# Mixing and base matmuls one tile further behind the attention, in code written out slot by slot

## What is computed

```python
# block 1: a low-rank adapter chosen per sample, then autocorrelation attention
u = einsum('bni,bri->bnr', x, B[id]); v = einsum('bnr,bor->bno', u, A[id])
f = rfft(v); corr = irfft(f * conj(f), n=1024)
weights, delay = top_k(corr, 6)                  # per row, over the 1024 lags
x = x + sum_k softmax(weights)[k] * roll(v, -delay[k])
# block 2: a 64x64 mix of the channels, chosen per sample, then a base layer with LoRA experts
m = einsum('bct,bcd->bdt', x, W[cond])
out = x + m @ W_base.T + b_base + 2.0 * top2_of_8_lora_experts(m)
```

## Time and profile before

| | us |
|---|---|
| median of 3 runs | 948.55 |
| lowest, highest | 946.2, 956.33 |
| span of the profiled execution | 948.1 |
| PE busy in it | 839.0 |
| DVE busy | 620.8 |
| POOL busy | 478.5 |
| ACT busy | 336.3 |

### The profile page before, as it was taken

One profiled execution on the slowest core, in us unless ns is written; L12 is line 12 of the kernel. 1 busy time (PEld: TensorE's weight loads), 2 busy tenths in 40 slices (PEclk: granted clock), 3 DMA queues, 4 the chain that ended last, 5 costly groups with the idle time before them and its releaser, 6 DMA issues. The chain is left out here.

```text
span 948.1 us, 16004 instructions
## 1 busy us (share of the span) xinstructions
PE 839.0 (88%) x4808; PEld 705.7 (74%) x4808; DVE 620.8 (65%) x1362; ACT 336.3 (35%) x617; POOL 478.5 (50%) x465
## 2 busy tenths in 40 slices
PE   4646899998998998998988989989989989999978
PEld 3645788777777787777877877777867778778766
DVE  2245667867677676766677576766667766777772
ACT  5343334233433333333442334333333333333311
POOL 1244544746575552755556355655337544555530
PEclk9856999999999999999999999999999989999998
DMA  8466576676766776665767667667666667777441
GB/s 277 140 195 203 185 232 213 211 239 197 232 201 203 237 240 185 212 217 184 234 202 242 192 195 214 194 208 226 193 209 194 206 212 223 234 235 234 166 146 45
DMA packets 66796, 194.48 MB, mean 205 GB/s; under 512 B 13708, under 2 KB 24236, under 8 KB 63540
## 3 DMA queue, kind: packets, MB, share of 16 engines
q0 software_dynamic: 23040, 83.90, 28.1%
q1 hardware_dynamic: 32084, 71.33, 26.8%
q10 hardware_dynamic: 11616, 38.67, 10.4%
HBM read 118.36 MB, written 50.33 MB: 178 GB/s over the span
## 5 line engine op out<-in xcount | busy, mean ns | idle before, releaser
L1093 POOL DMA_INDIRECT rolled<-y_d,off x160 | 168.6, 1054 | 297.9 <-DVE row L939 191.0
L939 DVE SCALAR_TENSOR_TENSOR row<-rolled,weight,row 128x1024 f32<-128x1024 f32 x160 | 226.5, 1416 | 101.7 <-DMA rolled<-y_d,off 98.6
L463 PE MATMUL o_ps<-wt_hi,x_hi 128*128 128x512 f32 x512 | 219.6, 429 | 0.0
L463 PE MATMUL o_ps<-wt_hi,x_lo 128*128 128x512 f32 x512 | 202.2, 395 | 0.0
L463 PE MATMUL o_ps<-wt_lo,x_hi 128*128 128x512 f32 x512 | 201.7, 394 | 0.0
L1082 POOL TENSOR_TENSOR row<-row,bias 128x1024 f32<-128x1024 f32 x32 | 77.7, 2427 | 88.1 <-PE x_ps L570 88.1
L570 PE MATMUL x_ps<-mix,row 128*128 128x128 f32 x512 | 76.5, 311 | 50.5 <-DVE row L939 32.6
L570 PEld LDWEIGHTS x_ps<-mix,row 128*128 128x128 f32 x512 | 70.4, 220 | 63.4 <-DVE row L939 38.2
L463 PEld LDWEIGHTS o_ps<-wt_hi,x_hi 128*128 128x128 f32 x512 | 96.6, 189 | 22.5 <-issue 4.8
L463 PEld LDWEIGHTS o_ps<-wt_hi,x_lo 128*128 128x128 f32 x512 | 96.2, 188 | 22.1
L463 PEld LDWEIGHTS o_ps<-wt_lo,x_hi 128*128 128x128 f32 x512 | 97.0, 189 | 14.6
(11 more groups left out here) (130 smaller groups left out, 1485.5 us busy)
## 6 DMA issues: line engine op xcount, KB each, us to landing
y_d<-y ACTq DMA_DIRECT2D x64, 512.0 KB, 3.6
row<-in_x SPq DMA_DIRECT2D x32, 512.0 KB, 7.0
adapter<-g_hi SPq DMA_DIRECT2D x64, 256.0 KB, 4.5
out<-row SPq DMA_DIRECT2D x32, 512.0 KB, 2.9
adapter<-g_lo SPq DMA_DIRECT2D x32, 256.0 KB, 4.5
r<-in_L_cond_A SPq DMA_DIRECT2D x72, 64.0 KB
r<-in_L_cond_B SPq DMA_DIRECT2D x56, 64.0 KB, 2.0
rolled<-in_L_ffn_W_base SPq DMA_DIRECT2D x5, 512.0 KB, 6.0
```

The lines of the kernel that those rows point to most:

```text
L463: last = pe.matmul(dst, a, b, start=start and n == 0, stop=stop and n == len(todo) - 1)
L939: dve.scalar_tensor_tensor(row[u][:, :], rolled[n % RB][:, :], weight[:, n:n + 1], row[u][:, :], ALU.mult, ALU.add).then_inc(sum_step, 1)
L1093: pool.indirect_dma_start(out=rolled[n % RB][:, :], out_offset=None, in_=y2_d[u], in_offset=bass.IndirectOffsetOnAxis(ap=off[:, n:n + 1], ...
```

## The change

LAG becomes 3. `base`, `experts`, `router`, `bias_added`, `out_add` and the store work on tile s-3. `mixed` and its copies work on m = s-2, where they stood on s-1. All keep their places in the slots, so `mixed(s-2)` stands where `mixed(s-1)` stood, in front of `correlation(s)`. There is one slot more, 34. A fifth row buffer holds the tile that is now kept longer, tile t in buffer t % 5. Its space comes from `ft`, which now lies in `r2`. The loop goes: all 35 slots are written out on all five engines, with constants in the waits. `load_mix` gets a wait on `x2_mm` of four tiles before.

```diff
-LAG = 2
+LAG = 3
 U = 4
+NROW = 5
...
-def wait_apart(eng, regs, holds, *waits):
...
-        row = [sb(f"row{u}", [P, L]) for u in range(U)]
+        row = [sb(f"row{n}", [P, L]) for n in range(NROW)]
...
+        ft = r2[:, 0:L].rearrange("p (k c) -> p k c", k=KC)
...
-        ft = sb("ft", [P, KC, P])
...
-        def slots(eng, slot):
-
-            for s in range(U):
-                slot(s, s % U, s // U)
-            with eng.Fori(1, NG - 1) as i:
-                for u in range(U):
-                    slot(i * U + u, u, i)
-            for s in range(NT - U, NT + LAG):
+        def slots(slot):
+            for s in range(NT + LAG):
                 slot(s, s % U, s // U)
...
             def load_mix(t, u):
+                if t >= U:
+                    sp.wait_ge(x2_mm, 2 * (t - U) + 2)
...
             def slot(s, u, i):
-                t, g = s - LAG, i + 1
+                t, m, g = s - LAG, s - LAG + 1, i + 1
...
-                if has(s - 1):
+                if has(m):
                     if prep and u == 0:
                         pe.wait_ge(at_out, 2 * g + 2)
...
-                    mixed(s - 1, *before(u, i, 1))
+                    mixed(m)
                 if attn:
                     correlation(s)
...
-                if has(last):
+                if has(m):
                     for h in range(2):
-                        act.wait_ge(x2_mm, 2 * last + 1 + h)
+                        act.wait_ge(x2_mm, 2 * m + 1 + h)
...
-                if has(last):
+                if has(m):
                     for h in range(2):
-                        dve.wait_ge(x2_h, 2 * last + 1 + h)
+                        dve.wait_ge(x2_h, 2 * m + 1 + h)
```

More of the change, by code:

```diff
@@ L239, in tiles @@
         b_in = sem("b_in")
-        row_in = [sem(f"row_in{u}") for u in range(U)]
+        row_in = [sem(f"row_in{n}") for n in range(NROW)]
         mix_in = [sem(f"mix_in{u}") for u in range(U)]
@@ L450, in _ @@
             load_a(1)
-            slots(sp, slot)
-            for u in range(U):
-                sp.wait_ge(out_saved[u], 16 * NT // U)
+            slots(slot)
+            for n in range(NROW):
+                sp.wait_ge(out_saved[n], 16 * len(range(n, NT, NROW)))
         @blk.tensor
@@ L620, in slot @@
                         base(t, c)
-                    if c < 2 and attn and not first(s):
-                        x_transposed(s, u, i, c)
-                    if c == 2 and attn and not first(s):
+                    if c < 2 and attn and s > 0:
+                        x_transposed(s, c)
+                    if c == 2 and attn and s > 0:
                         b_times_x(s, u, i)
@@ L626, in slot @@
                         pe.wait_ge(x2_l, 2 * t + 2)
-                    if c == (6 if first(s) else 2) and u == 0 and prep:
+                    if c == (6 if s == 0 else 2) and u == 0 and prep:
                         a_transposed(g)
@@ L630, in slot @@
                         h_transposed(t)
-                    if c == 3 and attn and not first(s):
+                    if c == 3 and attn and s > 0:
                         bx_repeated(s)
@@ L644, in slot @@
                         adapter_out(s, u)
-                    if first(s) and c in (4, 5):
+                    if s == 0 and c in (4, 5):
                         w_transposed(KC - 6 + c)
@@ L694, in _ @@
             pe.wait_ge(g_lo_sp, 1)
-            slots(pe, slot)
+            slots(slot)
         @blk.scalar
@@ L776, in slot @@
                                    accum_out=rsum[:, :]).then_inc(rexp_out, 1)
-                if attn and not first(s):
+                if attn and s > 0:
                     x_out(s, t)
-                if prep and u == 0 and not first(s):
+                if prep and u == 0 and s > 0:
                     a_out(g)
@@ L874, in _ @@
             w_high(5)
-            slots(act, slot)
+            slots(slot)
         @blk.vector
         def _(dve):
-            regs = [dve.alloc_register(f"dve_wait{n}") for n in range(2)]
             def low(dst, src, hi):
@@ L998, in slot @@
                     weights(last)
-                    add_y(last, ul)
-                if has_attn(s) and not first(s):
+                    add_y(last)
+                if has_attn(s) and s > 0:
                     bx_masked(s)
                 if has(last):
-                    add_rolled(last, ul, 0)
+                    add_rolled(last, 0)
                 if has(t):
@@ L1006, in slot @@
                     low(ht_lo[:, :], ht_ps, ht_hi[:, :]).then_inc(ht_l, 1)
-                if has_attn(s) and not first(s):
+                if has_attn(s) and s > 0:
                     stack_low(s)
-                if first(s):
+                if s == 0:
                     w_low(KC - 2)
@@ L1046, in _ @@
             w_low(5)
-            slots(dve, slot)
+            slots(slot)
         @blk.gpsimd
         def _(pool):
-            regs = [pool.alloc_register(f"pool_wait{n}") for n in range(3)]
             for u in range(U):
@@ L1137, in _ @@
             pool.wait_ge(bias_in, 16)
-            slots(pool, slot)
+            slots(slot)
 _INS = ["x", "itok_B_4_50", "itok_B_0_15", "L0_cond_A", "L0_cond_B", "L0_cond2_weights", "L0_ffn_W_base",
```

170 lines of the change are left out of this document (84 added, 86 removed).

## The result

| | us |
|---|---|
| after, median of 4 runs | 971.65 |
| lowest, highest | 967.8, 978.21 |
| before, beside it, median of 4 runs | 950.45 |
| after / before | 1.021, interval 1.016 to 1.026 |
| span of the profiled execution | 972.8 |

The change makes the kernel 2% slower. The prediction was 950, with a range of 928 to 961.

The account below looks back on a forecast made before the run. Bound: a ring of correlation, `top_delays`, gathers and rolled additions, with POOL's `powers`, `eo_hi`, `eo_lo` beside; PE's list nearly as long. Terms -13.0 - 1.0 + 1.1 + 0.6 + 4.2 - 2.8 - 1.2 + 13.9 = +1.8 gave 950 us, range 928 to 961.

Parts of the forecast that it names:

- the collision: POOL's bias addition, released sooner, runs before DVE's `eo_lo` instead of beside it and holds it up, 2.2 us.
- what would show it: Signs: no "issue" wait before L899, wait moved to `c_ps`, `eo_lo` some 3 us in slots 14, 18, 22, 26.
- Rival A: The idea works: `eo_lo` gets in before the bias addition; -20.7 us, 928 us, chance 0.22.
- Jumps and register waits, "-13.0 - 1.0": Written-out code removes DVE's stalls after five jumps, -13.0 us, and register waits before the first gather, -1.0 us.
- Rival C: DVE's "issue" stall isn't the jump's and stays in written-out code; 963 us, chance 0.05.
- Rival B: Written-out code stalls in its own instruction fetches, 2.7 us each; 1036 us at one a slot; chance 0.07.
- POOL isn't there earlier; nothing: Slots with u = 0: `folds` stands between `powers` and the bias addition, so no change.
- u = 2, "31.3 each, +1.1" and "slot 10 stays": Five slots with u = 2: 31.3 us each with 0.2 for the clock, +1.1 in all; slot 10 unchanged, `eo_lo` late anyway.
- Slots 28 to 31, "+4.2, between 0 and 8.4": Last slots without preparation: bias addition holds `eo_lo`, +2.1 us in slots 28 and 30; +4.2, between 0 and 8.4.
- u = 3, "+0.6": Slots with u = 3: slot 11 gives 0.6 us, slot 23 loses 1.2 by the bias addition holding `eo_lo`; +0.6.
- Front, "-2.8 - 1.2": Slot 1 loses its mixing, -2.8 us; slot 2 loses `base`, -1.2 us.
- Tail, "+13.9": One slot more after the last correlation: 56.8 us for 42.9, with 0.8 for the clock; +13.9 (+13 to +15).

Follow-up runs that it names:

- e2: Changed kernel with one more wait: POOL's bias addition goes behind `eo_lo`; 940.74 us, ratio 0.988 to the kernel before.
- e3: Changed kernel with a bias addition of one column instead of 1024; 938.68 us, ratio 0.987 to the kernel before.
- e1: Changed kernel with LAG = 2 again: written-out code and fifth buffer without the lag; 946.44 us, ratio 0.995 to the kernel before.
- e5: e2 with one more wait: DVE's last rolled addition waits until POOL's `powers` are done; 943.48 us, ratio 0.989 to the kernel before.
- e10: e9 with LAG = 2, so the same three orders without the lag; 914.27 us, ratio 0.959 to the kernel before.
- e7: Changed kernel with bias addition and `a_low` behind `eo_lo`, and last rolled addition behind `powers`; 932.0 us, ratio 0.978 to the kernel before.
- e9: e7 with the last rolled addition held behind `powers` only in slots with u = 1; 924.28 us, ratio 0.972 to the kernel before.
- e8: e1 with the last rolled addition waiting until POOL's `powers` are done; 942.62 us, ratio 0.990 to the kernel before.
- e4: Changed kernel with 26 unread transposes between mixing and correlation in six slots with u = 2; 963.64 us, ratio 1.012 to the kernel before.

## Why the prediction was wrong

**Where it failed.** The path and the collision that were forecast are the ones that came. What failed are sizes, two above all: the gain of the written-out code, put at -14.0, measured -5.9, and slots 28 to 31, put at +4.2 and at most 8.4, measured +11.5. Behind several terms stands one more, the clock after an idle stretch, allowed 0.2 a slot with u = 2, 0.8 in the tail and nothing elsewhere, and measured at 0.8 and 2.65 in the first two.

**The mechanism held.** The row was read rightly: the bias addition, released sooner, goes ahead of `eo_lo`, which takes 2.95 in slots 6, 10, 14, 18, 22 and 26; the wait moves to `c_ps`, as what would show it said; DVE has no "issue" wait over 0.3. e2 and e3 show that this is the cause. The rule of the Trainium skill, "GPSIMD Engine Reference", Specifications, that GpSimd shares its SBUF interfaces with VectorE and is contended by instructions with two SBUF inputs, agrees with all of these rows (2.95 against 0.81); the section says nothing on who goes first, and this alone is worth 31 us. Rival A is half right in this light: its order, forced by e2, is better by far than the forecast's, but it gave 941 and not 928: by the slots some 8 of the jumps' gain are missing, to which the second collision belongs, and 4.5 with u = 3.

**Jumps and register waits, "-13.0 - 1.0".** Mis-sized: u = 0 and u = 1 together gave -5.9. The stalls did vanish, 11.7 us in e1. Rival C fell with that.

Rival B fell too: in the changed kernel no "issue" wait of DVE or POOL is over 0.3. PE has one of 1.95 before its first mixing, in slot 2, in every kernel with LAG = 3; it wasn't looked into and is far from one a slot. Three of the other written-out kernels have a long one of POOL in front of a gather: 5.3 in slot 29 of e2 and e5, 7.75 in slot 23 of e10. They delay nothing: the same gather starts at 11.5 us of slot 29 there and at 11.3 in the kernel before, and at 13.8 of slot 23 in e10 and in the kernel before, where the profile puts its wait down to a rolled addition. Slot 23 is longer than its like in every kernel: 26.0 to 27.7 in the one before, the changed one and those with LAG = 2, 27.9 to 31.5 in e2 to e7 and e9, where the others with u = 3 mostly take 24 to 25. Why it grows in these stays open.

Two things took the gain back. The gathers, 0.47 us sooner, were priced "-1" with a lower bound of 0; an earlier start was taken to be no loss at worst. In e1 the slots with u = 1 came to +4.2, by the collision with `powers` that e5 and e8 take away again and by the clock in some of them. (In the changed kernel they came to -1.7.) And with the lag mixing is done early in the slots with u = 0 as well, PE idles before the correlation, and in four of them (4, 8, 12, 20) it then takes 2.8 to 3.3 where it took 1.9. Slot 4, "25.5" before, took 28.7: 1.4 by this, and 1.8 because its last rolled addition started 1.4 later, took 2.22 for 1.82 against POOL's folds, and `eo_lo` ended at 25.2 of the slot and not at 23.4. The prediction put these slots down as "POOL isn't there earlier; nothing": it looked at POOL and not at the clock.

**u = 2, "31.3 each, +1.1" and "slot 10 stays".** +3.2 in the five slots (158.6 for 155.4) and +1.9 in slot 10. The collision's 2.2 was right; where 0.2 had been allowed for the clock, 0.8 was measured (e4). Slot 10 had been left out because its `eo_lo` was late anyway; the new order made it as late as the others.

**Slots 28 to 31, "+4.2, between 0 and 8.4".** +11.5, beyond the bound. Two collisions of 2.1 were counted; there were three (slots 28, 30, 31: `eo_lo` of 2.96, 2.25 and 3.0), and the correlations after them took 3.3, 2.8 and 3.3 for 1.9, at the lower clock. With 2.1 and 1.4 that is up to 3.5 a slot. Slot 31 went further, from 24.0 to 28.4, and slot 29, without a collision, from 24.2 to 25.3. The prediction had seen that slots 29 and 31 miss the collision by 0.1 to 0.4 us only; its bound of 8.4 stood for a collision in all four slots. What went beyond that is the clock, for which it had put nothing here.

**u = 3, "+0.6".** +2.9. The term was made of -0.6 in slot 11 and +1.2 by a collision in slot 23. Slot 11 took 1.2 more (25.9 for 24.7): its `eo_hi` ended at 23.0 of the slot and not at 20.7, since two of POOL's `powers` took 1.73 and 1.71 beside rolled additions where one alone takes 0.73. In slot 23 `eo_lo` went first and took 0.81, and the slot took 26.0 for 26.2. The other slots are 0.2 to 0.6 longer each. All seven start at the lower clock, behind the wait in the slot before; what that costs them was not measured.

**Front, "-2.8 - 1.2".** -5.8 in slots 1 and 2, 1.8 better, against +1.7 of T0.

**Tail, "+13.9".** +15.2. base(30) was forecast at +22.0 and started at +21.7. What was too small is again the clock's term. The tail of the changed kernel in three windows, up to the start of base(30), to the end of its experts, and the rest:

```profile
914.80:936.50 21.70, 18.39 (x103) 15.72 (x102) 16.80 (x39) 3.12 (x9) 7.73 (x6) 0.97 0.39 122
936.50:953.00 16.50, 16.48 (x66) 13.38 (x67) 3.67 (x14) 0.71 (x4) 0.00 (x0) 0.83 0.08 33
953.00:972.80 19.80, 15.47 (x79) 12.61 (x77) 5.17 (x16) 2.69 (x7) 2.38 (x1) 1.00 0.13 53
```

After PE's wait of 3.33 us the granted clock is 0.83 for the stretch of base(30), and from its first matmul at 936.52 to the next mixing at 951.87 are 15.35 where 12.7 had been counted: +2.65, of which 0.8 was allowed.

**In sum.** The forecast's +1.8 became +24.8: +7.3 in the last slots, +8.1 of the jumps' gain lost, +4.1 with u = 2, +2.3 with u = 3, +1.3 in the tail, and -0.1 at the front (T0 included). One thing runs through several of them: an idle stretch of PE of some 3 us in front of a matmul train was priced at its length and a little for the clock, and in the two places where it could be read off it cost its length plus 0.8 (u = 2) and plus 2.65 (tail). How the clock and the collisions share in the u = 0, u = 1 and u = 3 slots stays open; only u = 2 was measured apart.

## What to carry to other kernels

Before work is moved earlier, list what it releases, and for each such instruction which other engine it was seen to hold up and what is due there at that time; an instruction released early can hold up the one that matters. Where two orders are possible, ask for the better one by a semaphore: here one wait was worth 31 us, and three of them with the written-out code and without the lag put the kernel 4% under the one before. And price a new idle stretch of TensorE by the rows of what follows one, not by its length alone; a deeper lag also pays its extra slot once (14 us here), whatever it saves per tile (here 1 us in one slot of four).

## What the runs showed of the hardware

- In the rows shown, a POOL addition and a DVE instruction with two SBUF inputs don't share the time; one runs whole, then the other, and the one that waits goes next, even between two additions of DVE: `eo_lo` 0.81 alone, 1.89 behind a fold of 1.27, 2.95 behind a bias addition of 2.4. A DVE addition with one input in PSUM runs on beside a bias addition, 1.23, where one with no bias addition beside it takes 1.21.
- A useless train of 26 transposes in a wait of some 3.8 us kept the granted clock at 1.00 and made the slot 0.8 us shorter (e4).
- A jump back cost DVE 13.3 / 5 = 2.7 us on average, 3.6 at most. The Trainium skill, "Runtime: NRT & Kernel Launch", Instruction fetch mechanics, holds that the fetch behind a taken branch to code not yet fetched is not hidden and that fetching straight on mostly is; the runs agree for DVE (11.7 us over five jumps gone in e1, and no such wait of DVE in its written-out slots).
